# Sturm recurrence: one scalar-operand pair of VectorE operations for each direction, in place of tables made on GpSimd

## The reference

```python
h = maximum(_layernorm(x), 0); x = x + L0(h, adj, ...)   # two graph convolutions, then LSTMs over windows of 1..4 nodes
h = maximum(_layernorm(x), 0); x = x + L1(h, adj, W, a)  # graph attention (GAT) with leaky scores
h = maximum(_layernorm(x), 0); x = x + L2(h, adj, Wqkv, Wo)  # causal attention with adj as additive mask
h = maximum(_layernorm(x), 0); x = x + L3(h, adj, W1, b1, W2, b2)
# L3, the spectral block:
deg = sum(A, 0) + sum(A, 1) - diagonal(A)
L_norm = d_inv_sqrt[:, None] * (diag(deg) - A) * d_inv_sqrt[None, :]
_, U = eigh(L_norm)                                      # 128 x 128
out = relu((U.T @ features) @ W1 + b1) @ W2 + b2
return U @ out
```

## Time and profile before

| | us |
|---|---|
| median of three runs (lowest, highest) | 965.54 (964.47, 966.66) |
| profiled execution: span | 962.9 |
| profiled execution: PE, DVE, ACT, POOL busy | 810.6, 758.1, 502.6, 168.7 |
| first Sturm pass, 633 to 717: DVE busy of 84 us | 66.58 |
| histogram of the first pass, 717 to 728: DVE busy of 11 us | 10.07 |
| second Sturm pass, 728 to 835: DVE busy of 107 us | 99.39 |
| 835 to 903: PE, DVE busy of 68 us | 57.68, 54.13 |
| 903 to 963: PE busy of 60 us | 55.99 |

### The profile page before, as it was taken

How to read it: one execution, slowest core, us unless ns; L and a number is a source line. 1 busy time by engine, 2 the same in 40 slices (tenths; PEclk the granted TensorE clock), 3 DMA queues, 4 the chain that set the end, 5 groups by cost and what they waited for, 6 DMA issues and landing times. The chain is left out here.

```text
span 962.9 us, 13676 instructions
## 1 busy us (share of the span) xinstructions
PE 810.6 (84%) x3862; PEld 535.5 (56%) x3862; DVE 758.1 (79%) x3165; ACT 502.6 (52%) x1106; POOL 168.7 (18%) x397
## 2 busy tenths in 40 slices
PE   4579998888999999999999997758882868889898
PEld 3468774434444466666555453736661655566565
DVE  6877777887888778888888888968989989869633
ACT  0037875554444434444433433148881776788675
POOL 2111111111111211211212120002202333071000
PEclk9999999999999979999999999879996988999999
DMA  9000000000000000000000000000000000000022
GB/s 281 14 1 1 2 1 1 1 1 0 1 1 0 1 1 1 0 1 1 2 0 1 1 1 0 1 0 1 1 1 1 1 0 1 1 1 1 22 77 77
DMA packets 13970, 12.16 MB, mean 13 GB/s; under 512 B 1092, under 2 KB 10823, under 8 KB 13895
## 3 DMA queue, kind: packets, MB, share of 16 engines
q1 hardware_dynamic: 10704, 8.46, 3.0%
q10 hardware_dynamic: 3190, 2.84, 1.0%
HBM read 7.10 MB, written 4.19 MB: 12 GB/s over the span
## 5 line engine op out<-in xcount | busy, mean ns | idle before, releaser
L565 ACT ACTIVATE G<-bank,bias 128x512 f32<-128x512 f32 (+1 forms) x252 | 158.6, 636 | 234.7 <-PE bank L662 197.1
L662 PE MATMUL bank<-HT,wih 128*128 128x512 f32 (+1 forms) x504 | 250.5, 583 | 0.5 <-ACT HT L551 0.5
L432 POOL TENSOR_TENSOR col_root<-sa,neg_half 128x1 f32<-128x1 f32 x126 | 79.5, 631 | 484.4 <-DVE sa L907 484.4
L662 PEld LDWEIGHTS bank<-VI 128*128 128x128 f32 x506 | 94.5, 202 | 120.2 <-DVE VI L905 57.8
L662 PE MATMUL bank<-H,whh 128*128 128x512 f32 (+1 forms) x288 | 136.2, 555 | 2.6 <-DVE H L905 2.6
L662 PE MATMUL bank<-VI 128*128 128x129 f32 (+63 forms) x506 | 95.4, 272 | 22.3 <-DVE VI L905 22.2
L521 ACT ACTIVATE T<-X,nbias,rstd 128x128 f32<-128x128 f32 x256 | 104.7, 487 | 5.1 <-DVE nbias L906 5.1
L525 ACT COPY T<-bank 128x512 f32<-128x512 f32 x128 | 75.0, 586 | 56.2 <-PE bank L662 41.8
L662 PEld LDWEIGHTS bank<-XI,A 128*128 128x128 f32 x252 | 41.1, 201 | 89.3 <-DVE A L906 87.5
L662 PEld LDWEIGHTS bank<-HT,wih 128*128 128x128 f32 x504 | 80.8, 195 | 10.3 <-issue 4.4
L672 PE MATMUL bank<-ident,T 128*128 128x128 f32 x256 | 40.7, 288 | 52.1 <-ACT T L608 43.4
(11 more groups left out here) (339 smaller groups left out, 1559.4 us busy)
## 6 DMA issues: line engine op xcount, KB each, us to landing
out_x<-T SPq DMA_DIRECT2D x16, 256.0 KB, 2.3
wih<-in_WihT ACTq DMA_DIRECT2D x1, 1024.0 KB
whh<-in_WhhT ACTq DMA_DIRECT2D x1, 1024.0 KB
qkvT<-in_WqkvT ACTq DMA_DIRECT2D x1, 192.0 KB
wg<-in_Wg ACTq DMA_DIRECT2D x2, 64.0 KB
l3w<-in_L3W ACTq DMA_DIRECT2D x2, 64.0 KB
adjT<-in_adjT ACTq DMA_DIRECT2D x1, 64.0 KB
adj<-in_adj SPq DMA_DIRECT2D x1, 64.0 KB, 2.1
```

The costliest lines, as they stand in the source:

```text
L432: e.tensor_tensor(out=col["root"][:, :], in0=sa[:, 0:1], in1=neg_half[:, :], op=ALU.pow).then_inc(root_ready, 1)
L565: e.activation(G[x.h][:, gate, 0:n], gate_bank(k)[:, 0:n], ACT.Tanh if gate == 2 else ACT.Sigmoid, bias=bias[:, 4 * (x.p - 1) + gate:4 * ( ...
L662: mm = lambda out, l, r, start=True, stop=True: e.matmul(out, l, r, start=start, stop=stop)
```

## The change

The recurrence takes d[s] and n2[s] as one value for each partition, a scalar operand of SCALAR_TENSOR_TENSOR: `t = (M - d) * p[s+1]` and `p[s+2] = p[s] * n2 + t`. A scalar operand holds for the whole instruction, and the two directions have different ones, so each direction has its own pair: four instructions of f elements to a step, in the order t forward, t backward, p forward, p backward. Each waits for the one two places before it (semaphore ch_r). The product `u[0]` at the opening of a block goes, as do GpSimd's `table`, its semaphore dl_ready and the function `tables`. GpSimd keeps the products. VectorE waits for m_ready, which its own computation of M increments, at the opening of each pass. p_done is incremented twice a block. At a pause the backward p increments lull, and VectorE waits for lull only before its second instruction behind the pause; before, it waited for lull ahead of the attention work.

```diff
--- before.py
+++ after.py
@@ -249,11 +249,6 @@
 LULLS = lulls()
 
 
-def tables(n):
-
-    return sum(len(CUTS[i // NB]) - 1 for i in range(n))
-
-
 def window_of_piece(b, j):
 
     return j if b < NB - 1 else j // 2
@@ -346,7 +341,6 @@
         CA8, CB8 = octet(lstm_weights[:, 0:2 * P]), octet(lstm_weights[:, 2 * P:4 * P])
         CT8 = [quad(lstm_weights[:, ds((4 + i) * P, P)]) for i in range(4)]
         HTf = HT[:, :, :, :].rearrange("p g t b -> p (g t b)")
-        DL = [g[:, :, :].rearrange("p a b -> p (a b)") for g in G]
         PB = [HTf[:, ds(2304 * i, 2304)] for i in range(2)]
         prod = HTf[:, ds(4608, 2048)]
 
@@ -358,8 +352,8 @@
         x_ready, a_ready, oh_ready, s_ready, gx_ready, sa_ready, root_ready, p_ready, k_ready, w_ready, wr_ready = sems(
             "x_ready a_ready oh_ready s_ready gx_ready sa_ready root_ready p_ready k_ready w_ready wr_ready")
         td_in, td_rep, wy_ps, wy_dv, wy_ac, lull = sems("td_in td_rep wy_ps wy_dv wy_ac lull")
-        m_ready, dl_ready, p_done, pr_ready, sgn_ready, sum_ps, hist_in, hist_ps = sems(
-            "m_ready dl_ready p_done pr_ready sgn_ready sum_ps hist_in hist_ps")
+        m_ready, p_done, pr_ready, sgn_ready, sum_ps, hist_in, hist_ps = sems(
+            "m_ready p_done pr_ready sgn_ready sum_ps hist_in hist_ps")
         lam_rdy, lam_ps, nrm_in, nrm_rt, z_rdy, z_ps, y_rdy, u_ps, u_sb = sems("lam_rdy lam_ps nrm_in nrm_rt z_rdy z_ps y_rdy u_ps u_sb")
         ch_e, ch_r, ch_n, ch_p, tw_in, tw_done = sems("ch_e ch_r ch_n ch_p tw_in tw_done")
         stats_in, rstd_rt, ln_rdy, pre_pe, pre_sb = sems("stats_in rstd_rt ln_rdy pre_pe pre_sb")
@@ -440,35 +434,21 @@
                 cuts = CUTS[ps]
                 pieces = [slice(lo, hi) for lo, hi in zip(cuts, cuts[1:])]
 
-                def table(b, j):
-                    n = ps * NB + b
-                    lo, size = cuts[j], cuts[j + 1] - cuts[j]
-                    e.tensor_tensor(out=v4(DL[n % 2], KB, f)[:, pieces[j]], in0=M[:, 0:f].unsqueeze(1).unsqueeze(1).to_broadcast([P, size, 2, f]),
-                                    in1=d2[:, ds(b * KB + lo, size), :].unsqueeze(3).to_broadcast([P, size, 2, f]), op=ALU.subtract).then_inc(dl_ready, 1)
-
                 def product(b, j):
                     pb = v4(PB[(ps * NB + b) % 2], KB + 2, f)
                     lo, size = cuts[j], cuts[j + 1] - cuts[j]
                     e.tensor_tensor(out=v4(prod, KB, f)[:, pieces[j]], in0=pb[:, ds(lo + 1, size)], in1=pb[:, ds(lo + 2, size)],
                                     op=ALU.mult).then_inc(pr_ready, 1)
 
-                e.wait_ge(m_ready, ps + 1)
-                if ps:
-                    e.wait_ge(p_done, ps * NB - 1)
-                for j in range(len(pieces)):
-                    table(0, j)
-                for b in range(NB):
+                for b in range(1, NB):
                     n = ps * NB + b
-                    if n:
-                        e.wait_ge(p_done, n)
-                    if b and n >= 2:
+                    e.wait_ge(p_done, 2 * n)
+                    if n >= 2:
                         e.wait_ge(sgn_ready, n - 1)
                     for w, window in enumerate(LULLS[n]):
                         e.wait_ge(lull, window[0])
-                        if b < NB - 1:
-                            table(b + 1, w)
                         for j in range(len(pieces)):
-                            if b and window_of_piece(b, j) == w:
+                            if window_of_piece(b, j) == w:
                                 product(b - 1, j)
             twist = Chain(e, ch_p)
             TP = lambda o, a, b, op: e.tensor_tensor(out=o, in0=a, in1=b, op=op)
@@ -1183,32 +1163,42 @@
                 two = lambda a: a[:, 0:2 * f].rearrange("p (c f) -> p c f", c=2)
                 for b in range(NB):
                     n = ps * NB + b
-                    pb, dl = v4(PB[n % 2], KB + 2, f), v4(DL[n % 2], KB, f)
-                    u, t = [two(a) for a in uu], two(tt)
-                    nbc = lambda s: n2[:, b * KB + s, :].unsqueeze(2).to_broadcast([P, 2, f])
+                    pb, t, shift = v4(PB[n % 2], KB + 2, f), two(tt), M[:, 0:f]
                     if b == 0:
                         if n:
                             e.wait_ge(pr_ready, products(n - 1))
+                        e.wait_ge(m_ready, ps + 1)
                         rec.note(e.memset(pb[:, 0], 0.0))
                         rec(e.memset(pb[:, 1], 1.0))
-                    rec(TT(u[0], pb[:, 0], nbc(0), ALU.mult))
+                    forth = back = rec.n
+                    paused = False
                     for s in range(KB):
-                        if s in CUTS[ps]:
-                            e.wait_ge(dl_ready, tables(n) + 1 + CUTS[ps].index(s))
-                        k = rec.note(TT(t, pb[:, s + 1], dl[:, s], ALU.mult))
-                        if s < KB - 1:
-                            rec.note(TT(u[(s + 1) % 2], pb[:, s + 1], nbc(s + 1), ALU.mult))
-                        e.wait_ge(ch_r, k)
+                        d_s, n_s = [d2[:, b * KB + s, k:k + 1] for k in range(2)], [n2[:, b * KB + s, k:k + 1] for k in range(2)]
                         half_next = half_behind(ps, b * KB + s)
-                        if s == KB - 1:
-                            TT(pb[:, s + 2], t, u[s % 2], ALU.add).then_inc(p_done, 1)
-                            e.wait_ge(p_done, n + 1)
-                        elif half_next:
-                            pauses += 1
-                            TT(pb[:, s + 2], t, u[s % 2], ALU.add).then_inc(lull, 1)
+                        e.wait_ge(ch_r, forth)
+                        forth = rec.note(STT(t[:, 0], shift, d_s[0], pb[:, s + 1, 0], ALU.subtract, ALU.mult))
+                        if paused:
                             e.wait_ge(lull, pauses)
                         else:
-                            rec(TT(pb[:, s + 2], t, u[s % 2], ALU.add))
+                            e.wait_ge(ch_r, back)
+                        back = rec.note(STT(t[:, 1], shift, d_s[1], pb[:, s + 1, 1], ALU.subtract, ALU.mult))
+                        paused = half_next > 0 and s < KB - 1
+                        e.wait_ge(ch_r, forth)
+                        ahead = STT(pb[:, s + 2, 0], pb[:, s, 0], n_s[0], t[:, 0], ALU.mult, ALU.add)
+                        if s < KB - 1:
+                            forth = rec.note(ahead)
+                        else:
+                            ahead.then_inc(p_done, 1)
+                        e.wait_ge(ch_r, back)
+                        behind = STT(pb[:, s + 2, 1], pb[:, s, 1], n_s[1], t[:, 1], ALU.mult, ALU.add)
+                        if s == KB - 1:
+                            behind.then_inc(p_done, 1)
+                            e.wait_ge(p_done, 2 * n + 2)
+                        elif paused:
+                            behind.then_inc(lull, 1)
+                            pauses += 1
+                        else:
+                            back = rec.note(behind)
                         for _i in range(half_next):
                             attentions(halves)
                             halves += 1
```

## The result

The changed kernel takes 968.73 us (median, 968.22 to 970.06), the kernel before 965.53 (964.47 to 966.66): ratio 1.0038, interval 1.0024 to 1.0053. A second measurement (e7) gave 1.0043 (1.0027 to 1.0059). The forecast of 962.9 was wrong, and the time lies just outside the range. The profiled execution took 968.51 us with a span of 966.4, against 965.5 and 962.9.

A forecast was written before the change was run, and what follows sets the result against it. VectorE sets the second pass's pace; in the first, VectorE, ScalarE and TensorE hold each other. First pass +2.8, second -5.5, total -2.7 on the 962.9 span: 960.2, plus 2.6 for the median, 962.9 us; range 955.5 to 968.5.

The forecast's parts named there:

- Five pauses begin earlier: First pass: attention's first operation no longer waits for the sum, 0.160 behind it in place of 0.25; -0.5 us.
- Twelve pauses begin 0.319 - 0.194 = 0.125 earlier: Second pass: pauses start sooner, -1.5 us; one lost at 812 us behind GpSimd's products, leaving -1.4.
- Distance binds in both: Both passes: instruction distance, not latency, prices a step; 0.640 against 0.528 us (first), 0.776 against 0.733 (second).
- The 13 slower steps at the end of the first pass: From 693 us: their +1.5 us falls into VectorE's waits of 0.36, 0.91 and 1.85, so costs nothing.
- The wait of 0.88: First pass: VectorE's wait for products set going a pause earlier shrinks behind six slower steps; -0.6 us.
- Opening and dm: Second pass: without table collisions the opening gains -3.2 us and dm in the first pause -1.0.
- The late products: Second pass: products start earlier without tables; -0.4 at 759.89, -1.0 at 786.41, -1.2 for the wait ending ScalarE's chain.
- Double waits: Block openings: the first forward instruction is held by two waits, +0.07 us each; +0.2 a pass.
- rival 3: Table gains smaller through other waits or new collisions; -1.2, -1.0 and half of -1.4 fail; 965.5 us, 10%.
- 1 (the load hides): Recurrence, both passes: scalar load costs nothing, latency binds a step at 0.574 and 0.640 us; 954 us, 13%.
- 4 (halved rate): Recurrence: two non-bf16 SBUF sources halve throughput, +33 and +67 ns an instruction, 22 us; 985 us, 2%.
- 2 (the load does not overlap with two SBUF streams): Some 400 recurrence instructions: each extra ns costs 0.4 us; 20 ns give 970, no overlap 996 us; 17%.

The follow-up runs named there:

- e7: The changed kernel, unaltered, measured a second time: 968.80 us, 1.0043 of the kernel before.
- e13: The changed kernel with spare matmuls (results unused) in TensorE's idle times between 885 and 902 us: 967.27 us, 1.0025 of the kernel before.
- e14: As e13, with spare matmuls also in TensorE's idle times in the first pass: 967.52 us, 1.0029 of the kernel before.
- e2: First pass as changed (scalar pairs, no tables), second pass as in the kernel before: 971.53 us, 1.0065 of the kernel before.
- e3: The kernel before with its old recurrence, but GpSimd makes no tables and M - d is left out: 959.56 us, 0.9936 of the kernel before.
- e4: The changed kernel with GpSimd still making all tables, awaited but never read: 975.42 us, 1.0099 of the kernel before.
- e8: The changed kernel with constants 0.5 and -0.25 in place of the scalars loaded from SBUF: 949.35 us, 0.9835 of the kernel before.

## Why the prediction was wrong, step by step

- **Pauses counted twice (1.9 us).** The failed step is "Five pauses begin earlier", priced at 5 x -0.09, and "Twelve pauses begin 0.319 - 0.194 = 0.125 earlier". The pause does begin one distance behind the last instruction; but the step was priced as four distances, and this holds to the pause as well. In the trace the interval of six steps and a pause grew from 6.05 us (673.19 to 679.24) to 6.77 (675.90 to 682.67), by 0.73 = 6 x 0.122, and in the second pass five steps and a pause from 6.52 to 6.78, by 0.26 = 5 x 0.052. Nothing is saved at the pause: the latency I subtracted was never in the sum. The first pause operations of that interval, two lines of before and two of after:

```profile
673.19 0.69 DVE L1029 TENSOR_REDUCE sm<-T 128x4 f32<-128x512 f32 x1
...
679.24 0.69 DVE L1029 TENSOR_REDUCE sm<-T 128x4 f32<-128x512 f32 x1
```

```profile
675.90 0.68 DVE L1009 TENSOR_REDUCE sm<-T 128x4 f32<-128x512 f32 x1
...
682.67 0.68 DVE L1009 TENSOR_REDUCE sm<-T 128x4 f32<-128x512 f32 x1
```

- **Distances too small by 2 ns (0.8 us).** 0.1625 and 0.196 against 0.160 and 0.194: 33 x 0.010 = 0.3 and 59 x 0.009 = 0.5. They lie within the bounds given (0.168 and 0.202); four times per step they still count. "Distance binds in both" was right.
- **The 13 slower steps at the end of the first pass.** That their +1.5 "fall into them" holds in the main where the clock is full: +0.3 us is left in e7, +0.4 in e13, +0.8 in e14. In the first trace 2.2 is left, beside half clock.
- **The wait of 0.88 (-0.6 forecast).** It went whole, -0.85, in the first trace of the change, in e2 and in e14, where TensorE was at full clock. In e7 and e13 it shrank by 0.45 only, beside half clock at 687 to 691 and 689 to 693 us; this is the wait in e7:

```profile
690.06 0.61 DVE L886 SCALAR_TENSOR_TENSOR X<-bank,sm,X 128x128 f32<-128x128 f32 x2 [0.43 <-PE bank L642]
```

- **The sum of the first pass,** in the order forecast, pauses, distance, this wait, last steps: 2.8 + 0.5 + 0.3 - 0.25 + 2.2 = 5.55 in the first trace, 2.8 + 0.5 + 0.3 - 0.25 + 0.8 = 4.15 in e14, 2.8 + 0.5 + 0.3 + 0.15 + 0.4 = 4.15 in e13.
- **Opening and dm:** 4.1 us against 4.2, right; e3 and e4 show that the tables were the cause. **The late products:** the t at 759.89 came out 0.36 shorter (0.4), the stretched operations at 786 0.9 (1.0), the wait at 780 1.1 to 1.3 (1.2), right. Not foreseen: the last count waits 1.31 instead of 0.96 us, +0.35. Second pass 3.1 in the first trace and 2.9 in e7, e13 and e14, instead of 5.5: 1.4 for the pauses, 0.5 for the distance, 0.35 for the count, the rest in tenths.
- **Double waits** 0.07 each, right.
- **The end.** The forecast carried the search's shift unchanged to the end ("whatever the search loses or gains arrives at the end, less what waits absorb"). It does in e3. In the other traces with an altered search 0.5 to 3.4 us were added behind the last count (e2: -0.2), beside half clock; with spare matmuls it was -0.9 to +0.7. This was in no term; rival 3 had thought of waits for TensorE, but within the passes, and not of its clock.
- **Rivals.** 1 (the load hides) is refuted by the steps, and e8 shows what it would have been: distances of 0.1125 and 0.136. The estimates of 0.11 and 0.14, worked out from the Trainium skill, "Vector Engine (DVE) Microarchitecture Reference", section 5.2, agree with these distances with immediates, and not with the 0.1625 and 0.196 with scalars from SBUF. 4 (halved rate) is refuted: 32 more elements cost 0.034 us an instruction. 2 (the load does not overlap with two SBUF streams) is refuted in its hard form, while its price, 0.4 us per ns, explains the 0.8. 3 fell by its reason: the -1.2 and the -1.0 held, and the -1.4, which did fail, and whole, is the pauses counted twice and not a wait.

In sum the terms of the first trace: 2.8 (first pass) + 2.4 (second) + 0.5 (behind) + 0.6 (an offset that the execution had ahead of the search) = 6.3 us, where forecast and span are 6.2 apart (-2.7 and +3.5).

## What to carry to other kernels

Price a chain of short instructions by start-to-start distances, and then do not subtract at its end a latency that the sum never held. An operand that is a column in SBUF is not free: here three instructions over both halves, with a broadcast tensor and a ready table, beat four with scalars (a step of 0.528 and 0.733 us against 0.650 and 0.785), although each reads more. And a gain on one engine is safe only if the engine behind it keeps its clock: check the granted clock in more than one trace before you book it.

## What the runs showed of the hardware

- A scalar taken from SBUF adds 0.050 us (32 elements) and 0.060 us (64) to the distance of two scalar_tensor_tensor in SBUF; with immediates the distance is 0.1125 and 0.136 (the change and e8).
- VectorE's scalar form with two SBUF sources collides with GpSimd's tensor_tensor as the plain form does: 2.42 us for a pair of 0.48 (e4). The Trainium skill, "Advanced Engine Details and Errata", section "GPSIMD Details", names such conflicts for VectorE instructions with two SBUF inputs; the trace agrees.
- TensorE's clock fell to half at changing places. In e7 TensorE had idle times of 1.65 and 0.68 us in the five us ahead of the one at 895.5; ahead of the X at 705.29 us it had idle times of 2.01 and 0.93 us and kept full clock. Beside a fall a wait of VectorE was 0.5 to 1.7 us longer than before (2.5 in e8). With spare matmuls in the idle times at 885 to 902 us the clock stayed full from 867 to 950 us in all five traces, four of them with an altered search. What decides whether it falls was not found.
